# Cross-attention and a 32-expert FFN on one core: gate and up matrices dealt to the partitions four rows at a time

## What is computed

```python
x = x + xattn(layernorm(x), ctx)                 # 8 heads of 64, 64 context rows per batch
X = layernorm(x).reshape(-1, 512)                # 16384 tokens
scores = sigmoid(X @ gate_w.T)
_, idx = top_k(scores + bias, 4)                 # E = 32 experts, K = 4
...                                              # each expert keeps its first C = 512 tokens
xe = gathered rows of X                          # (32, 512, 512)
h = silu(einsum('ecd,edi->eci', xe, W1)) * einsum('ecd,edi->eci', xe, W3)   # i = 256
ye = einsum('eci,eid->ecd', h, W2)
out = x + sum over the 4 experts of w * ye + silu(X @ sw1.T) * (X @ sw3.T) @ sw2.T
```

## Time and profile before

| | us |
|---|---|
| median of 3 runs | 1765.45 (1762.36 to 1768.41) |
| span of the profiled execution, which is all of its own time that is given | 1810.0 |
| expert stage in it, from the first gather to the end | 1323.0 to 1810.0 |
| last transposes of PE in it | 1754.5 |

### The profile page before, as it was taken

One profiled execution on the slowest core, in us unless ns is written; L12 is line 12 of the kernel. 1 busy time (PEld: TensorE's weight loads), 2 busy tenths in 40 slices (PEclk: granted clock), 3 DMA queues, 4 the chain that ended last, 5 costly groups with the idle time before them and its releaser, 6 DMA issues.

```text
span 1810.0 us, 31933 instructions
## 1 busy us (share of the span) xinstructions
PE 1641.8 (91%) x9056; PEld 1023.7 (57%) x9056; DVE 1378.9 (76%) x3486; ACT 1066.3 (59%) x2368; POOL 1252.4 (69%) x1104
## 2 busy tenths in 40 slices
PE   6999999999999999999999999999447999999991
PEld 4565656666566665656666565655224555555550
DVE  4678988987898897889779789898425777777771
ACT  4777766776776676777767767765213444444440
POOL 2337777777777777777767677777475787777874
PEclk8999999999999999999999999999678999999996
DMA  7557876667776666677666577777249889988665
GB/s 247 144 135 166 193 163 151 174 155 154 181 183 152 162 168 155 174 167 178 164 149 170 152 182 171 161 191 170 61 142 264 139 172 166 208 190 167 103 85 79
DMA packets 474532, 293.75 MB, mean 162 GB/s; under 512 B 342643, under 2 KB 385397, under 8 KB 474356
## 3 DMA queue, kind: packets, MB, share of 16 engines
q1 hardware_dynamic: 429300, 239.03, 51.9%
q0 software_dynamic: 45056, 52.67, 18.5%
HBM read 135.06 MB, written 110.17 MB: 135 GB/s over the span
## 4 chain that ended last, share of the span: by engine, by line
PE 45%; issue 17%; DVE 16%; ACT 9%; another core or an unknown queue 4%; DMA 3%; POOL 2%; SPq 2%; DVEq 0%; ACTq 0%; POOLq 0%
PE O_ps L500 9%; PE S_ps L485 8%; PE GE_ps L1580 5%; PE UE_ps L1580 4%; PE G_ps L527 4%; PE YE_ps L1620 4%; PE U_ps L527 3%; PE PREP_ps L583 2%; POOL out L1557 2%; PE PREP_ps L566 2%; DVE top_s L1280 2%; DVE x_l L1221 1%; DMA pt_l<-p_l 1%; PE TE_ps L1606 1%
## 5 line engine op out<-in xcount | busy, mean ns | idle before, releaser
L923 POOL DMA_INDIRECT slot_table<-tok_line,slot x480 | 507.7, 1058 | 132.0 <-issue 128.1
L932 POOL TENSOR_TENSOR xt_l<-xt,xt_h 128x512 fp32r<-128x512 f32 x128 | 164.6, 1286 | 179.5 <-ACT xt_h L758 179.5
L799 ACT ACTIVATE prob<-S_ps,rs 128x512 f32<-128x512 f32 x128 | 88.0, 688 | 257.3 <-DVE S_ps L1286 166.5
L485 PE MATMUL S_ps<-a_h,xt_h 128*128 128x512 f32 x512 | 213.3, 417 | 2.4 <-DVE m_l L1259 2.4
L500 PE MATMUL O_ps<-m_h,pt_h 128*128 128x512 f16 x512 | 195.9, 383 | 20.0 <-DMA pt_l<-p_l 18.9
L485 PE MATMUL S_ps<-a_h,xt_l 128*128 128x512 f32 x512 | 202.1, 395 | 0.0
L485 PE MATMUL S_ps<-a_l,xt_h 128*128 128x512 f32 x512 | 202.0, 395 | 0.0
L500 PE MATMUL O_ps<-m_h,pt_l 128*128 128x512 f16 x512 | 194.7, 380 | 0.0
L500 PE MATMUL O_ps<-m_l,pt_h 128*128 128x512 f16 x512 | 194.6, 380 | 0.0
L947 POOL TENSOR_TENSOR prob<-prob,rsum 128x512 f32<-128x512 f32 x128 | 135.4, 1058 | 83.0 <-DVE rsum L1314 62.3
L1557 POOL DMA_INDIRECT out<-ye,idx_far x80 | 126.3, 1579 | 52.2 <-issue 27.7
(11 more groups left out here) (245 smaller groups left out, 4848.8 us busy)
## 6 DMA issues: line engine op xcount, KB each, us to landing
xt<-in_xT SPq DMA_DIRECT2D x128, 256.0 KB
xr<-in_x SPq DMA_DIRECT2D x64, 512.0 KB, 3.8
x2aug<-x SPq DMA_DIRECT2D x128, 256.0 KB
out<-xr SPq DMA_DIRECT2D x64, 512.0 KB, 3.2
up_more<-in_w SPq DMA_DIRECT2D x36, 256.0 KB
slot_table<-tok_line,slot POOLq DMA_INDIRECT x512
up_w<-in_w SPq DMA_DIRECT2D x28, 256.0 KB
down_more<-in_w SPq DMA_DIRECT2D x18, 256.0 KB
```

Of the source, the lines that this page charges most:

```text
L485: last = pe.matmul(S_ps[t % 2][:, :], left[:, kc, :], right[:, b % 2, kc, :], start=(m == 0), stop=(m == 3 * KD - 1))
L799: act.activation(prob[:, t % 2, :, :], S_ps[t % 2][:, :].rearrange("p (h j) -> p h j", h=H), ACT.Exp, scale=rs[:, q % 2, 0, t % 2:t % 2 + ...
L923: pool.indirect_dma_start(table, bass.IndirectOffsetOnAxis(ap=slot[:, g % 2, i, q:q + 1], axis=0), tok_line[:, g % 2, i, :], None, bounds_ ...
L932: pool.tensor_tensor(xt_l[:, t % 2, :, :], xt[:, t % 2, :, :], xt_h[:, t % 2, :, :].bitcast(F32), ALU.subtract).then_inc(xt_lo, 1)
```

## The change

The rows of W1 and W3 are dealt to the partitions four neighbours at a time: partition p holds rows 4p to 4p + 3. Four rows of 256 bf16 values are then 2 KB in one piece, both in DRAM and, since gate and up now have a half of the set each, in SBUF; before, they were four pieces of 512 B. So that the sum over features still pairs the right rows, block kc of a turned chunk has to hold features kc, kc + 4, kc + 8 and so on: each transpose reads every fourth column of `rows`, values that lie 16 B apart. W2 stays as it is. The numbers of instructions of all engines, their order and their waits stay as they are; the DMAs for gate and up keep their number and bytes and change form.

```diff
-    up_w = sb("up_w", [P, 4, KD, 2 * I], BF16)
+    up_w = sb("up_w", [P, 4, 2, KD, I], BF16)
...
-    up_more = sb("up_more", [P, WEIGHT_SETS - EARLY_SETS, KD, 2 * I], BF16)
+    up_more = sb("up_more", [P, WEIGHT_SETS - EARLY_SETS, 2, KD, I], BF16)
...
-    up_src = [w.rearrange("e (c p) i -> e p c i", p=P) for w in (w1, w3)]
+    up_src = [w.rearrange("e (p c) i -> e p c i", p=P) for w in (w1, w3)]
...
         for n in range(2):
-            sp.dma_start(up_set(e)[:, :, n * I:(n + 1) * I], up_src[n][e]).then_inc(set_loaded[r], 16)
+            sp.dma_start(up_set(e)[:, n], up_src[n][e]).then_inc(set_loaded[r], 16)
...
-        def up_half(bank, e, w0, c):
+        def up_half(bank, e, w, c):
...
-                    last = pe.matmul(bank[:, :], up_set(e)[:, kc, w0 + c * P:w0 + (c + 1) * P],
+                    last = pe.matmul(bank[:, :], up_set(e)[:, w, kc, c * P:(c + 1) * P],
                                      part[:, e % TURNED, kc, :], start=(n == 0), stop=(n == 2 * KD - 1))
...
-            up_half(UE_ps[c], e, I, c).then_inc(ue_done, 1)
+            up_half(UE_ps[c], e, 1, c).then_inc(ue_done, 1)
...
             for kc in range(KD):
                 last = pe.transpose(TE_ps[i % 2][:, kc * P:(kc + 1) * P].bitcast(F32R),
-                                    rows[:, e % RING, i, kc * P:(kc + 1) * P], ident_r[:, :])
+                                    rows[:, e % RING, i, 0:D].rearrange("p (d k) -> p k d", k=KD)[:, kc, :], ident_r[:, :])
             last.then_inc(t_done, 1)
```

## The result

The change makes the kernel slower by 0.28%: the ratio to before is 1.0028, with a 95% interval of 1.0020 to 1.0037. The medians are 1769.23 us (20 runs, of which two at 2764.27 and 9322.57 stand apart) and 1762.91 us for before (20 runs). I had forecast 1763.0, a gain of 2.5 us, so the sign is wrong. The size is just under the 0.3% that I took for the bound, but the interval excludes no change.

The account below looks back on a forecast made before the run. The prediction took the PE ramp up to about 1400 us and then POOL's chain as the bound, PE having 17.7 us of slack. Terms -2.3 - 1.0 + 0.8 = -2.5 us gave 1763.0 us, range 1754 to 1783.

Parts of the forecast that it names:

- the 0.3% that I took for the bound: Smallest difference in run time to be told from no change, about 0.3% (5.3 us).
- What bounds the kernel: Expert stage: PE ramp to about 1400 us, then POOL's chain sets the end; PE has 17.7 us of slack.
- 8.1 us of longer steps: PE's 27 steps from 5 to 32, each 0.30 us longer by strided transposes; less than the slack, so no cost.
- the weakest place: Profiled execution 44.6 us over the median; if other runs lack PE's slack, the transposes count in full.
- The steps of 13.50 us: POOL's 19 steps from 1397.28 to 1653.77 us, while weights load; without a wait a step takes 12.81 to 12.86.
- the 9.9 us of waits: POOL's waits that go with the weights, 19 x (13.50 - 12.98); packets were to shrink them by 2.3 us.
- The 1.0 us that I took for the ramp: Gain from cheaper packets up to about 1400 us, taken from a 1.46 us wait before POOL's scatter at 1397.28.
- Packets: Gate and up loads in 2 KB packets: 10.7 engine-us less per expert, 0.67 us on 16 engines.
- the 3.3 us of gain expected: Gains from packets: 2.3 us of POOL's waits in loading steps and 1.0 us in the ramp.
- Transposes: PE's strided weight loads: some 25 ns more each, 12 of 16 exposed a step; 0.8 us net cost, in the ramp.
- The second: Rival at L1606: strided load, +85 ns, makes PE the bound; 9 to 19 us slower, middle 1779; chance 0.29.
- From 10 ns on, if there is no slack: Threshold of the strided-load rival without PE slack; 46 ns gives 12 x 31 x 0.046 = 17 us less 3.3, 1779.

Follow-up runs that it names:

- base: The unchanged kernel before, profiled once more after the first profile of 1810.0 us; span 1761.5 us, own time 1763.34 us.
- the second pair: The kernel before and the changed kernel, each profiled once more; own times 1761.93 and 1769.54 us.
- the first four and the next five profiles of the last table: Profiles without strided transposes in third and fourth groups, against five with them; expert 4 to last scatter 391.0 against 397.1 us in the mean.
- base2: The unchanged kernel before, profiled yet again; span 1760.1 us, own time 1761.93 us.
- packets_only: Changed kernel with contiguous transposes, so only gate and up come in 2 KB packets (wrong rows paired); 0.9994 (0.9984 to 1.0004) of before.
- stride_covered: Kernel before with strided transposes in the first and second group of a step only; 1.0000 (0.9988 to 1.0012) of before.
- stride_exposed: Kernel before with strided transposes in the third and fourth group of a step only; 1.0024 (1.0016 to 1.0033) of before.
- after_psum: Changed kernel with the hidden product kept in PSUM, so `he_l` has one SBUF input; 1.0004 (0.9993 to 1.0014) of before.
- before_psum: Kernel before with the hidden product kept in PSUM, so `he_l` has one SBUF input; 0.9977 (0.9967 to 0.9986) of before.

## Why the prediction was wrong

*What bounds the kernel.* This is the step that failed: that POOL's chain runs by itself 17.7 us behind PE, so that 8.1 us of longer steps are covered. The number was right, even in a usual execution: in `base` the last `ye` of expert 28 and its scatter are, in the timelines of DVE and POOL,

```profile
1695.00 0.74 DVE L1729 TENSOR_SCALAR ye<-YE_ps,rows 128x512 f32<-128x512 f32 x1
...
1713.69 1.54 POOL L1557 DMA_INDIRECT out<-ye,idx_far  x1 [0.30 <-issue]
```

17.9 us apart after the 0.75 of the instruction. In the changed kernel they are

```profile
1704.92 0.74 DVE L1729 TENSOR_SCALAR ye<-YE_ps,rows 128x512 f32<-128x512 f32 x1
...
1721.79 1.54 POOL L1557 DMA_INDIRECT out<-ye,idx_far  x1 [0.30 <-issue]
```

16.1 apart. Had the slack been there to spend, 27 steps at 0.44 us would have taken 11.9 of it and left 6. In this pair they took 1.8, and in the second pair 3.8 (19.0 to 15.2). At the last scatter, which is what the time depends on, the lag fell by 2.1 us between the means of the first four and the next five profiles of the last table, while PE's loop grew by 8.2; the difference came out as time. A gap between two loops is slack only if the second can close it; here POOL's own step is as long as PE's (12.86 and 12.77 us), and late in the stage it is held by DVE once a step when PE's step is the longer one. Nor was the gap PE's to spend: POOL also feeds PE, with the gathers, and PE already waited for them. I had both facts in view: the two step lengths, and a scatter of 1.73 us behind one of 1.62, which I did not ask about.

*The profile I read.* I named as the weakest place that the profiled execution was 44.6 us over the median, and that with no slack in the other runs the transposes would count in full. That condition was not what happened, since the lag was there, but about half of the 11.9 us came through all the same. The steps of 13.50 us, and with them much of the 9.9 us of waits that the packets were to shrink, belonged to that execution: from the scatter of expert 8 to that of expert 20 it took 13.70 us a step, `base` 12.86 and `base2` 13.01. The 1.0 us that I took for the ramp had no row behind it: the wait of 1.46 us at 1397.28 is marked "issue", not DMA.

*Packets.* Right in sign at most, and some six times too large. The set fell from 43.4 to 41.6 engine-us, not by 10.7; the price of a 2 KB packet, taken from stores, was the wrong row. The share fell from 0.91 to 0.84 (0.85 was forecast), but that is luck: the fall is in the gathers and scatters, not in the weights. Of the 3.3 us of gain expected, `packets_only` shows 1 us with an interval that holds zero; 3.3 us, 0.19%, lies outside it.

*Transposes.* I put 25 ns between ends of 0 and 85; it is 57, nearer to the 46 of the ordinary four-byte load, which was the nearest row and which I halved for no reason that a row gave. Of the groups I held 12 loads exposed; 8 are, as the wait for `xe_l` covers the first group as well as the second. 8 x 57 ns is 0.46 us a step, where I had 0.30 (measured: 0.44).

*The rivals.* The second, that the strided load makes PE the bound, is what happened: loads 144 ns apart (I had asked for over 110) and a slower kernel. But its path to the end was not the one that I gave: PE's step stayed under 13.4, no scatter waited long for `ye` late in the stage, and the slack was never used up. With 57 ns it would have given 57 - 55 = 2 ns beyond the slack, near to nothing; the loss was 5 us (0.28%). "From 10 ns on, if there is no slack" gave the right kind of answer, and 8 x 31 x 0.057 = 14 us would have been three times the loss.

*What stays open.* That the loss comes with the 8 exposed loads is shown by `stride_covered` and `stride_exposed`, and that it is the growth of PE's loop less what POOL's lag gives back is shown by the sums above. Why the lag gives back only 2 us is shown in part: the hold by `he_l` is real late in the stage, but without it `after_psum` still takes 4.1 us more than `before_psum`, with a loop 9.4 us longer and a lag 5.3 shorter. What else keeps POOL from closing up in the steps before expert 20 is open.

**The best version** is `before_psum`: the old weights and transposes, and the hidden product in PSUM. It takes 0.9977 (0.9967 to 0.9986) of before, 1760.27 us in the median of 12 runs.

## What to carry to other kernels

The distance between two loops is slack only where the later loop is the faster one and nothing that it shares with the others holds it once a round; if both have the same step, price a longer step of the first in full, less the waits that it already has for the other (here some 3 to 4 of 11.9 us). If the profiled execution is far from the median, take a second one before you build on a wait in it. A stride moved from one engine to another has a price there too (here 57 ns on a weight load of 128 values per partition, 0.5 us on an ACT instruction of 512), so ask first whether the gain that it is to buy, here at most 3 us of transfers that nobody waited for, is on the path.

## What was not expected of the hardware

- A weight load of 128 x 128 float32r values takes 141 ns if they are contiguous, 195 if they lie 8 B apart and 198 if 16 B; in a group two follow each other after 86, 141 and 144 ns (medians).
- ACT's scaling of 128 x 512 float32 values takes 803 ns, 1309 if it reads 16 B apart and 1287 if it writes its values 512 B apart in turn.
- Weights in packets of 2 KB instead of 512 B took 41.6 instead of 43.4 engine-us for a set of 0.75 MB, and no time that could be measured.
- An indirect DMA instruction of POOL that starts while DVE has a 0.68 us instruction with two SBUF inputs is longer by 0.34 to 0.41 us (1.89 to 1.96 instead of 1.55); with one input in PSUM none of 80 was over 1.64. Keeping one of two inputs in PSUM gave 0.23% here for four lines.
